# Two of five key chunks of the probabilities turned by VectorE blocks and SBUF-to-SBUF transfers instead of TensorE

## The reference, cut to what matters

```
q = x @ Wq.T   (32 heads of 128);  k, v = x @ Wk.T, x @ Wv.T   (8 heads of 128)
q, k = rope(rmsnorm(q)), rope(rmsnorm(k))
k_all = concat(k_cache[block_table] (512 rows), k (128 rows))      # 640 keys; v_all likewise
scores = q @ k_all.T / sqrt(128), cached keys beyond cache_seqlens masked
o = softmax(scores) @ v_all;   x = x + o @ Wo.T
```

## Time and profile before

| what | value |
|---|---|
| three runs | 1352.56, 1352.72 and 1351.93 us, median 1352.56 |
| profiled execution: span from first to last instruction | 1349.8 us; the page gives no other time of it |
| the median run less this span | 2.8 us |
| a round of the attention | 16.60 us |
| PE busy | 1342.4 us, 99% of the span |
| DVE, ACT, POOL busy | 1040.8, 843.2, 713.6 us (77, 62, 53%) |
| granted TensorE clock | 1.00 of full speed |

### The profile page before, as it was taken

How to read it: one execution, slowest core, us unless ns; L and a number is a source line. 1 busy time by engine, 2 the same in 40 slices (tenths; PEclk the granted TensorE clock), 3 DMA queues, 4 the chain that set the end, 5 groups by cost and what they waited for, 6 DMA issues and landing times.

```text
span 1349.8 us, 24930 instructions
## 1 busy us (share of the span) xinstructions
PE 1342.4 (99%) x7812; PEld 1191.3 (88%) x7812; DVE 1040.8 (77%) x2131; ACT 843.2 (62%) x2217; POOL 713.6 (53%) x972
## 2 busy tenths in 40 slices
PE   9999999999999999999999999999999999999999
PEld 8888888888889998889888989888888888888887
DVE  7988777877787778777877787778778887748546
ACT  7676566666566556666666666566665785545444
POOL 7767465646554655565555555555555652305111
PEclk9999999999999999999999999999999999999999
DMA  5566325522552264126413641364222164354532
GB/s 201 172 185 198 87 82 173 145 63 78 187 127 59 78 201 134 38 84 206 130 31 108 203 109 31 113 210 128 79 48 48 63 191 140 125 183 141 187 141 78
DMA packets 170746, 168.11 MB, mean 125 GB/s; under 512 B 129856, under 2 KB 137664, under 8 KB 159936
## 3 DMA queue, kind: packets, MB, share of 16 engines
q1 hardware_dynamic: 164928, 131.21, 33.3%
q0 software_dynamic: 5760, 36.18, 8.1%
HBM read 133.81 MB, written 33.55 MB: 124 GB/s over the span
## 4 chain that ended last, share of the span: by engine, by line
PE 98%; POOL 1%; DVE 1%; ACT 1%; issue 0%; POOLq 0%; DVEq 0%
PE ps L64 27%; PE ps L63 27%; PE ps L65 27%; PE ps L1131 10%; PE ps L1109 2%; PE ps L1153 1%; PE ps L2038 1%; PE ps L1103 1%; PE ps L2071 0%; PE ps L2070 0%; PE ps L2024 0%; PE ps L2023 0%; PE ps L1332 0%; DVE at_scores L897 0%; PE ps L2009 0%; ACT at_mask L601 0%
## 5 line engine op out<-in xcount | busy, mean ns | idle before, releaser
L502 POOL TENSOR_SCALAR at_probs<-at_probs,at_row_inv 128x640 f32<-128x640 f32 x256 | 211.8, 828 | 151.1 <-DVE at_row_inv L903 150.9
L605 ACT ACTIVATE at_pT_hi<-ps 128x512 fp32r<-128x512 f32 x320 | 186.5, 604 | 101.1 <-PE ps L65 50.9
L897 DVE CUSTOM_DVE_ANT_0 at_scores<-ps,at_mask,at_inv_rms 128x640 f32<-128x640 f32 x256 | 220.2, 879 | 31.7 <-PE ps L65 30.8
L653 ACT ACTIVATE at_probs<-at_scores,at_neg_max 128x640 f32<-128x640 f32 x256 | 211.9, 836 | 51.0 <-DVE at_neg_max L897 51.0
L845 DVE TENSOR_TENSOR at_pT_lo<-ps,at_pT_hi 128x512 fp32r<-128x512 f32 x320 | 212.6, 686 | 25.7 <-ACT at_pT_hi L605 20.7
L63 PE MATMUL ps<-ds_hi,x_hi 128*128 128x512 f32 (+1 forms) x564 | 192.7, 342 | 0.0
L65 PE MATMUL ps<-ds_hi,x_lo 128*128 128x512 f32 (+1 forms) x564 | 192.0, 340 | 0.0
L648 ACT ACTIVATE at_square<-ps 128x128 bf16<-128x128 f32 x256 | 67.1, 276 | 166.7 <-DVE a_raw L876 149.9
L1131 PE MATMUL ps<-ident,at_probs 128*128 128x128 f32 x1280 | 160.6, 273 | 0.0
L63 PE MATMUL ps<-at_kT_hi,ds_lo 128*128 128x320 f32 x512 | 158.1, 309 | 1.6 <-DVE at_neg_max L897 1.6
L65 PE MATMUL ps<-at_kT_hi,ds_lo 128*128 128x320 f32 x512 | 158.2, 309 | 0.0
(11 more groups left out here) (215 smaller groups left out, 3379.6 us busy)
## 6 DMA issues: line engine op xcount, KB each, us to landing
kT_pages<-shared SPq DMA_DIRECT2D x16, 1024.0 KB
kv_raw<-kT_pages SPq DMA_DIRECT2D x60, 256.0 KB, 4.0
v_pages<-shared SPq DMA_DIRECT2D x14, 1024.0 KB
kv_raw<-v_pages SPq DMA_DIRECT2D x56, 256.0 KB, 4.1
sw_wgu_raw<-in_sw_gu SPq DMA_DIRECT2D x22, 512.0 KB, 3.3
staging<-in_L_cond_Wo SPq DMA_DIRECT2D x8, 1024.0 KB, 4.8
staging<-in_L_cond_Wq SPq DMA_DIRECT2D x7, 1024.0 KB
sw_b_raw<-in_sw_bgu SPq DMA_DIRECT2D x88, 64.0 KB, 2.8
```

What stands on the lines that cost most here:

```text
L502: pool.tensor_scalar(probs[:, h, :], probs[:, h, :], row_inv[:, h:h + 1], 1.0, ALU.mult, ALU.mult).then_inc(probs_done, 1)
L605: act.activation(out, src, ACT.Copy).then_inc(done, 1)
L653: act.activation(probs[:, h, :], scores[h % 2][:], ACT.Exp, bias=neg_max[:, h:h + 1], scale=-1.0, accum_out=row_sum[:, h:h + 1]).then_inc( ...
L897: dve.tensor_tensor_reduce(out=scores[h % 2][:], in0=slot(h), in1=mask[:, b, :], scale=inv_rms[b % 2][:, h:h + 1], scalar=3.0e38, op0=ALU. ...
```

## The change

For 62 of the 64 rounds (`by_moves`; not the first and not the last) chunks 3 and 4 are no longer turned by TensorE into PSUM. VectorE transposes the 32x32 blocks of each head's last 256 columns (`turn_squares`, one instruction of 128x256 float32 for each head, 4 a round) into a tile `turned`, and SP issues 16 transfers of 32 partitions by 1 KB (`move_turned`) that put the blocks where they belong in a tile `pT_raw`. `hi` and `lo` of the two chunks read `pT_raw` in SBUF where they read PSUM.

With it several orders change. ScalarE does the high part of chunk 3 between the first two exponentials and that of chunk 4 ahead of the third. VectorE does the low part of chunk 3 after the first `inverse`, that of chunk 4 after the second, and `mask_and_max` of head 3, an `inverse` and two `turn_squares` ahead of `attended`. TensorE does `score` of heads 2 and 3 ahead of `times_v` of chunks 3 and 4. SP's list begins each round with `move_turned`, ahead of all its loads and stores. GpSimd's page gather moves ahead of `rotate_k`. Three semaphores that only count passed waits become one, two others become one, and the scratch space for GpSimd's descriptors is set to 8192.

```diff
+            def turned_in_psum(g, b, c):
+                first = isinstance(g, int) and (g, b) == (0, 0)
+                return c + 1 if first else upto(g, b, KC - MOVED, MOVED + c + 1)
+            def moved_chunk(c):
+                return pT_raw[:, :, c - (KC - MOVED)].rearrange("p a h r -> p h a r")
...
+            def move_turned(g, b):
+
+                wait_apart(sp, turned_done, upto(g, b, G), passed)
+                for a in range(NQ):
+                    for k in range(NQ):
+                        sp.dma_start(pT_raw[k * SQ:(k + 1) * SQ, a], turned[a * SQ:(a + 1) * SQ, k]).then_inc(pT_moved[b % 2], 16)
...
                 for b in range(B):
                     g2, b2 = following(*following(g, b))
+                    if by_moves(g, b):
+                        move_turned(g, b)
                     if last and b == 0:
...
+                    if by_moves(g, b):
+                        probs_T(g, b, 3)
+                    if more:
                         exps(g1, b1, 1)
+                    if by_moves(g, b):
+                        probs_T(g, b, 4)
+                        exps(g1, b1, 2)
...
                     hi(oT_hi[:], bank(o_bank(b)), pv_done, upto(g, b, KC, KC), oT_hi_done)
...
+            def turn_squares(g, b, h):
+
+                wait_apart(dve, probs_done, upto(g, b, G, h + 1), passed)
+                dve.transpose(turned[:, :, :, h, :].rearrange("p k c r -> p c k r"),
+                              probs[:, h, (KC - MOVED) * P:KEYS].rearrange("p (c k i) -> p c k i", c=MOVED, k=NQ)).then_inc(turned_done, 1)
...
                         inverse(g1, b1, 0)
+                    if by_moves(g, b):
+                        probs_T(g, b, 3)
...
                     if more:
                         mask_and_max(g1, b1, 2)
                         inverse(g1, b1, 1)
+                    if by_moves(g, b):
+                        probs_T(g, b, 4)
+                        mask_and_max(g1, b1, 3)
+                        inverse(g1, b1, 2)
+                        if by_moves(g1, b1):
+                            turn_squares(g1, b1, 0)
+                            turn_squares(g1, b1, 1)
                     attended(g, b)
...
+                    if more and by_moves(g1, b1):
+                        turn_squares(g1, b1, 2)
...
+                    if more and by_moves(g1, b1):
+                        turn_squares(g1, b1, 3)
                     add_y(g, b, last)
...
-                    for c in range(2, KC):
+                    for c in range(2, KC - MOVED if by_moves(g, b) else KC):
                         probs_T(g, b, c)
...
                     times_v(g, b, 2)
-                    times_v(g, b, 3)
-                    if more:
+                    if by_moves(g, b):
                         score(g1, b1, 2)
-                    times_v(g, b, 4)
-                    if more:
                         score(g1, b1, 3)
+                        times_v(g, b, 3)
+                        times_v(g, b, 4)
...
-    nc = bacc.Bacc("TRN2", target_bir_lowering=False, num_devices=1)
+    nc = bacc.Bacc("TRN2", target_bir_lowering=False, num_devices=1, dynamic_dma_scratch_size=8192)
```

More of the change, by code:

```diff
@@ L245, in attention @@
         pT_done = sem("pT_done")
+        turned_done = sem("turned_done")
+        pT_moved = [sem(f"pT_moved{j}") for j in range(2)]
         pv_done = sem("pv_done")
@@ L287, in following, with by_moves, moved_count @@
             return (g, b + 1) if b + 1 < B else (g + 1, 0)
+        def by_moves(g, b):
+            return not (isinstance(g, int) and (g, b) in ((0, 0), (HK - 1, B - 1)))
+        def turned_in_psum(g, b, c):
[3 more added lines that the diff above has]
+            return pT_raw[:, :, c - (KC - MOVED)].rearrange("p a h r -> p h a r")
+        def moved_count(g, b):
+            return g * (B // 2 * NQ * NQ * 16) + (b // 2 + b % 2) * NQ * NQ * 16
         def project_bank(g, b):
@@ L544, in group @@
                         key_scale(g2, b2)
+                    if first and 2 <= b < 6:
+                        stage_pages(g, b - 2)
+                    if not first and not last and 1 <= b < 5:
+                        stage_pages(g, b - 1)
                     if b == B - 3 and not last:
@@ L554, in group @@
                         stage_first_keys(1)
[L555 to L558, removed]
                     if more2 and not (last and b == B - 3):
@@ L658, in probs_T @@
                     act.wait_ge(pv_done, upto(g, b, KC, c - RING + 1))
-                hi(pT_hi[c % RING][:], bank(probs_bank(b, c)), pT_in_psum, upto(g, b, KC, c + 1), pT_hi_done[c])
+                if by_moves(g, b) and c >= KC - MOVED:
+                    hi(pT_hi[c % RING][:].rearrange("p (h a r) -> p h a r", h=G, a=NQ), moved_chunk(c), pT_moved[b % 2], moved_count(g, b), pT_hi_done[c])
+                else:
+                    hi(pT_hi[c % RING][:], bank(probs_bank(b, c)), pT_in_psum, turned_in_psum(g, b, c), pT_hi_done[c])
             def new_keys(g, b):
@@ L729, in group @@
                         dense.part_hi(act, 0, 1)
-                    for c in range(3, KC):
-                        probs_T(g, b, c)
+                    if not by_moves(g, b):
+                        for c in range(KC - MOVED, KC):
+                            probs_T(g, b, c)
                     if last and b == B - 2:
@@ L759, in group @@
                     hi(oT_hi[:], bank(o_bank(b)), pv_done, upto(g, b, KC, KC), oT_hi_done)
-                    if more:
+                    if more and not by_moves(g, b):
                         exps(g1, b1, 2)
@@ L1201, in group @@
                     if more:
-                        pe.wait_ge(pT_done, upto(g, b, KC, KC))
+                        pe.wait_ge(pT_done, upto(g, b, KC, KC - MOVED if by_moves(g, b) else KC))
+                        if by_moves(g, b) and keys_by_row(g, b + 1):
+                            pe.wait_ge(kc_done, b + 2)
                         score(g1, b1, 1)
                     times_v(g, b, 2)
-                    times_v(g, b, 3)
-                    if more:
+                    if by_moves(g, b):
                         score(g1, b1, 2)
-                    times_v(g, b, 4)
-                    if more:
                         score(g1, b1, 3)
+                        times_v(g, b, 3)
+                        times_v(g, b, 4)
+                    else:
+                        times_v(g, b, 3)
+                        if more:
+                            score(g1, b1, 2)
+                        times_v(g, b, 4)
+                        if more:
+                            score(g1, b1, 3)
                     if more3:
```

58 lines of the change are left out of this document (32 added, 26 removed).

## The result

| | before | after |
|---|---|---|
| runs (median) | 1351.93 to 1353.58 us (1352.64) | 1651.94 to 1662.33 us (1657.38) |
| ratio, 95% interval | | 1.2253 [1.2226, 1.228] |
| profiled execution: its time, its span | span 1349.8 us | 1651.94, 1650.1 us |
| a plain round | 16.60 us | 20.4 us (20.1 to 20.9) |
| PE busy | 1342.4 us, 99% | 1432.1 us, 87% |

The forecast was 1453 us with a range of 1408 to 1503. The sign was right, the size was not: +305 us where +100 stood.

A forecast was written before the change was run, and what follows sets the result against it. TensorE, 98% of the chain, was taken to bound the kernel, with a chain behind it just in cover. 60 rounds x 1.23 = 74, + 8 + 18 = 100 us on 1352.6 gave 1453 us, range 1408 to 1503.

The forecast's parts named there:

- What is removed: TensorE loses 8 of 20 transposes a round, 0.87 us a round, 54 us over 62 rounds.
- the chain of a round: From `project_q` through exponentials and low parts to the output: 1.65 us of waits, a plain round 0.78 us longer.
- Port: Low part of chunk 3 on VectorE meets GpSimd's `normalise` at SBUF: delay 0.45 us, plain round 17.83.
- rival 1: The transfers are late: at 0.61 us an issue chunk 3 comes at 11.05, no port delay, 1523 us; chance 0.20.
- VectorE's transposes: Two before the output's low part, taken as covered at 0.35 us each; at 0.57 they cost 0.4 a round.
- The 16 transfers: SP issues at 0.455 us each, all landed at 8.7 us, before ScalarE wants them at 9.47: no cost.
- the ring over `project_q`: Closed cycle of a round through `project_q`, `turn_q`, squares, exponentials and value products: plain round 17.38 us before the port delay.
- Moved and added orders: Reordered work on VectorE and SP: 8 us in 14 rounds b = 0 and b = 5, +9 twice in the last group.
- the rounds with the single waits: Last group: late `dense.w` in round 2 and `loads.pick` delaying mask rows from round 6, +9 us each.
- Rounds b = 5: One more VectorE weight subtraction between chunk 3's low part and `mask_and_max` of head 2 adds 0.60 us.
- Rivals 2 to 4: Chain alone, 1408 to 1426 us (0.17); waits fall into cover, 1299 (0.07); gain and waits cancel, within 0.2% (0.03).

The follow-up runs named there:

- e1: The changed kernel without the 16 transfers, chunks 3 and 4 read from `turned` and so not fully transposed: 1494.8 us.
- e10: The changed kernel without transfers, chunk 3 ahead of the first exponential and inverse, chunk 4 ahead of the second, last transpose early, third exponential and inverse later: 1453.8 us.
- e6: The changed kernel with the fourth `turn_squares` directly behind the third, ahead of values and keys: 1556.8 us.
- e4: The changed kernel with 24 idle transposes on TensorE ahead of value product 3 in groups 1 to 7: 1664.2 us.
- e5: The changed kernel with SP's dense weights and register reads issued ahead of the transfers in the last group: 1640.8 us.
- e8: The changed kernel with the blocks written to DRAM in one transfer and read back in four, 5 issues a round: 1558.7 us.

## Why the prediction was wrong

- **What is removed; the chain of a round.** Right. In e1 every step comes within 0.4 us of the forecast: product 0 at 2.01 (1.95), first exponential 8.80 (8.66), output 15.38 (15.05 with the port), next round 18.2 (17.83). Most of the rest is that the first of three passes behind a gap (product 0, product 4, output) holds the chain 0.12 longer each time: 626.05 to 626.86 for product 4 in e1, where 0.69 is usual.
- **Port.** Right: 0.50 where 0.45 stood. The low part was held until 0.16 us before GpSimd's end, as in the earlier trace rows. The Trainium skill ("SBUF — State Buffer", section "SBUF: two separate sides") lets the later instruction wait for the earlier one's end; that would have been 0.66 here. Direction right, a little less measured. In the changed kernel `normalise` of head 0 is long through by then and the low part takes 0.69, as rival 1 had it.
- **VectorE's transposes.** Right to take them as covered in this order: 0.37 each in a pair. e10 shows that the cover is thin.
- **The 16 transfers: the step that failed.** I took 0.455 us an issue, from the two `Wq` loads, over 0.61 from four others, "as its addresses are fixed". It is 0.635, above my upper bound, and in 62 rounds. Chunk 3 comes at 11.65 instead of 8.7, 2.0 us too late, and the transfers that I had put at nothing cost 163 us, the changed kernel's 1657.4 less e1's 1494.8. The margin was 0.7, and I gave the later row a chance of 0.20. That an issue is cheaper because its addresses are fixed was a guess: the addresses of the 16 are fixed, and they cost more.
- **What a late transfer costs.** Also missed, in rival 1: I let the lateness add once (19.0) and did not close the ring. SP's first issue depends on the last transpose, and that stands, in VectorE's order, behind values and keys, whose `project_kv` TensorE does behind the late value products. I had checked the ring over `project_q` and not the one over SP. e6 shows it: 100 us for one line.
- **TensorE's clock.** In no step. Behind the gap of 2.48 us the products are 0.43 apart, where 0.23 is usual, the lower of the two levels (1.2 GHz); three and three of them cost 1.2 us, and the granted clock of the round is 0.92. It lengthens the ring, by 0.9 by e4. That its removal alone brings nothing was my third error, on record in e4's expectation.
- **Moved and added orders.** The rounds with the single waits: +11.7 and +10.4 where +9 and +9 stood. The second came near by luck, as only 5 of it are the wait for the mask rows (e5). Rounds b = 5: +2.3 to +2.9 and not 0.6. In round 4 the loads for sequence b + 2 stand behind SP's issues and the next group's weights and land late (6.93 us from issue to landing, on the chain above). In e1, where SP issues no transfers of blocks, most rounds b = 5 take 0.6 more than a plain one (18.85). Not foreseen: where the hardware loop starts again VectorE stands still for about 2.5 us. In the changed kernel little of it shows, as rounds b = 0 take 20.9; in e1 it costs the 24 us named above.
- **Rivals.** Rival 1's mechanism held, with a time (1523) that was 134 too low, for the ring and the clock. That it deserved more than 0.20 is the lesson of the issue price. Rivals 2 to 4 fell.

## What to carry to other kernels

A transfer that is issued in many small pieces costs its issuer's time, piece by piece. Before such a change, follow the ring over the issuing queue too: what the first issue waits for, and what that instruction stands behind on its own engine. Where the margin is smaller than the spread of the nearest rows, do not bet on the early case: price both, and give the late one a like chance. Once a ring decides, look for the instruction that is ready but queued: moving one line gave back 100 us here, where halving the bytes gave 10.

## What the runs showed of the hardware

- An issue on SP took 0.635 us for 32 partitions by 1 KB or by 512 bytes between two tiles in SBUF; in e8 0.34 for the single 512 KB write, and up to 0.47 for 32 partitions by 4 KB from DRAM. What makes an issue between two SBUF tiles the dearer one no run shows.
- A 128x256 float32 transpose in 32x32 blocks took VectorE 0.44 us, two in a row 0.75.
- VectorE stalls where the hardware loop starts again, 2.2 to 2.9 us in most of the runs with the change (3.5 in e8, 1.6 to 1.8 in e10). The kernel before shows no such stall, and 28 packets in instruction queue q14; the kernels with the change have 79 to 83 packets, and the stall. The changed kernel's page (packets, MB, share) and its timeline:

```profile
q14 instruction: 82, 0.67, 0.1%
```

```profile
708.17 1.29 DVE L885 TENSOR_TENSOR at_pT_lo<-ps,at_pT_hi 128x512 fp32r<-128x512 f32 x2 [2.45 <-issue]
```

That VectorE's instructions are fetched anew there, as its loop got longer, fits both numbers; I did not test it by a shorter loop.
